# Sampling in two image halves with TensorE's part as a four-step loop, and the token norm inside the stages

## What is computed

```python
off = conv_general_dilated(x, offset_w, window_strides=(16, 16), ...)   # 2 x 256 numbers for each patch
py, px = base_y + dy, base_x + dx
y0, x0 = floor(py), floor(px)
sampled = gather(y0, x0) * (wy0 * wx0) + gather(y0, x1) * (wy0 * wx1) \
        + gather(y1, x0) * (wy1 * wx0) + gather(y1, x1) * (wy1 * wx1)
out = einsum('bhwkc,ock->bohw', sampled, Wk)                             # 192 channels
```

## Time and profile before

| | |
|---|---|
| median of 3 runs | 1202.0 us (1199.74 to 1213.42) |
| the profiled execution | 1193.13 us, span 1191.0 us, mean granted clock 0.831 |
| PE busy | 896.0 us, 75% of the span |
| DVE busy | 528.9 us, 44% |
| ACT busy | 331.6 us, 28% |
| POOL busy | 265.5 us, 22% |

### The profile page before, as it was taken

One profiled execution on the slowest core, in us unless ns is written; L12 is line 12 of the kernel. 1 busy time (PEld: TensorE's weight loads), 2 busy tenths in 40 slices (PEclk: granted clock), 3 DMA queues, 4 the chain that ended last, 5 costly groups with the idle time before them and its releaser, 6 DMA issues. The chain is left out here.

```text
span 1191.0 us, 30855 instructions
## 1 busy us (share of the span) xinstructions
PE 896.0 (75%) x13348; PEld 756.5 (64%) x13348; DVE 528.9 (44%) x1178; ACT 331.6 (28%) x668; POOL 265.5 (22%) x289
## 2 busy tenths in 40 slices
PE   8888885699729981789866595687869999286593
PEld 5676662588618971577755473565469999265472
DVE  2367672454343316555532356453641111455364
ACT  0255550221202210244541133342201111143132
POOL 2266660231022421322200101110122223200100
PEclk9899998677758995899986598785868999688598
DMA  6344436800064901000001500000518992100000
GB/s 207 66 122 128 127 96 175 223 13 1 1 195 121 208 17 57 1 2 2 2 1 38 142 4 2 2 2 1 146 48 200 238 240 38 31 3 2 1 4 22
DMA packets 56553, 87.16 MB, mean 73 GB/s; under 512 B 10390, under 2 KB 43074, under 8 KB 56414
## 3 DMA queue, kind: packets, MB, share of 16 engines
q1 hardware_dynamic: 51294, 80.26, 26.2%
q0 software_dynamic: 5120, 4.88, 2.2%
HBM read 78.35 MB, written 7.30 MB: 72 GB/s over the span
## 5 line engine op out<-in xcount | busy, mean ns | idle before, releaser
L1677 PE MATMUL ps_rows<-stage_strip,stage_hat_y 64*32 64x96 f32 x3200 | 55.0, 255 | 19.2 <-issue 18.1
L2607 DVE TENSOR_TENSOR L_ffnhid<-L_ffnact_gate,L_ffnbank_u 128x300 f32<-128x300 f32 x32 | 14.9, 467 | 117.7 <-ACT L_ffnact_gate L2625 117.7
L1745 DVE TENSOR_TENSOR stage_product<-ps_rows,stage_hat_x 128x960 f32<-128x960 f32 x40 | 46.3, 1158 | 42.6 <-PE ps_rows L1677 41.7
L1662 PE MATMUL ps_places<-stage_rel_y,stage_spread 100*64 100x128 f32 x800 | 57.9, 291 | 5.7 <-issue 3.4
L1677 PEld LDWEIGHTS ps_rows<-stage_strip,stage_hat_y 64*32 64x32 f32 x3200 | 42.0, 108 | 30.3 <-issue 30.1
L1710 POOL TENSOR_SCALAR stage_hat_x<-stage_hat_x 128x320 f32<-128x320 f32 x40 | 51.1, 1279 | 42.5 <-ACT stage_hat_x L1701 42.5
L1662 PEld LDWEIGHTS ps_places<-stage_rel_y,stage_spread 100*64 100x64 f32 x800 | 47.2, 145 | 13.4 <-issue 8.4
L1699 ACT ACTIVATE stage_hat_y<-ps_places,stage_w_minus_row 128x640 f32<-128x640 f32 x40 | 31.8, 794 | 59.8 <-PE ps_places L1662 59.8
L1718 POOL TENSOR_TENSOR stage_hat_x<-stage_rel_x,stage_w_column 128x160 f32<-128x160 f32 x80 | 37.5, 490 | 39.1 <-POOLq L1503 39.1
L1750 DVE TENSOR_REDUCE stage_samples<-stage_product 128x120 f32<-128x960 f32 x40 | 45.7, 1144 | 0.0
L2540 POOL DMA_INDIRECT stage_y_rows<-L_ffndown,stage_choice_index x16 | 25.4, 1589 | 89.2 <-ACT L_ffndown L2632 46.9
(11 more groups left out here) (432 smaller groups left out, 2244.8 us busy)
## 6 DMA issues: line engine op xcount, KB each, us to landing
stage_strip<-in_strips SPq DMA_DIRECT2D x80, 189.0 KB, 3.4
L_ffn_win<-in_L_ffn_Win SPq DMA_DIRECT2D x10, 1152.0 KB, 10.8
stage_L_ffn_win<-in_L_ffn_Win SPq DMA_DIRECT2D x6, 1152.0 KB, 10.7
L_ffnranks<-stage_ranks SPq DMA_DIRECT2D x16, 400.0 KB, 4.6
L_ffn_win<-in_L_ffn_Win SPq DMA_DIRECT2D x8, 768.0 KB, 13.5
L_ffn_wout<-in_L_ffn_Wout SPq DMA_DIRECT2D x10, 576.0 KB, 9.3
stage_L_ffn_wout<-in_L_ffn_Wout SPq DMA_DIRECT2D x6, 576.0 KB, 10.7
L_ffn_wout<-in_L_ffn_W SPq DMA_DIRECT2D x8, 384.0 KB, 13.8
```

The lines of the kernel that those rows point to most:

```text
L1662: mm = nc.tensor.matmul(ps_places[HALF_P * h:HALF_P * (h + 1), i % 2, g * P:(g + 1) * P], k.spread[:, ho * GRID + g, :], k.rel_y[:, t, h * ...
L1677: mm = nc.tensor.matmul(ps[out, i % 2, h, g * cols:(g + 1) * cols], hat_y[rows, p, g, out], strip[rows, p, :, :, left:left + WINDOW_X].rea ...
L1745: nc.vector.tensor_tensor(products(i % 2), in_psum(i % 2), weights_x(i % BUFFERS), ALU.mult).then_inc(s["multiplied"], 1)
```

## The change

1. **Order of the steps.** The 40 steps go by halves of the images, then by patch row, then by the four tiles of the half, instead of by patch row and all eight tiles. The tokens are laid out in the order of the steps.
2. **Tiles of the row places.** `convolve_y` makes tiles of 80 tokens (the 4 steps of a group) instead of 100: ten tiles instead of eight, five in each half.
3. **PE's steps as a loop.** PE's program has a loop of ten passes with four steps each instead of 40 steps written out. Its waits compare with numbers made from the loop counter. So that the instructions of a pass can be the same, SP copies the 80 x 256 places of the coming group by DMA into one of two buffers, `own_y`; PE spreads from there. The last pass spreads two steps that nobody uses. The other engines' steps stay written out.
4. **Flag.** DVE reads `far` at once, the other engines behind their steps, in the same block: the barrier and the second block are gone. The far body has 4 steps instead of 20, in one more loop.
5. **Token norm.** `finish_norm` is gone. DVE aggregates the statistics of a tile one tile later, within the last block of the layer (`count`, `end_count`), and ACT ends that block with `root`: logarithm, then exponential with scale -0.5, after asking for the table that holds both. The mean is read in place. `attention` asks for this table at its start in all its kinds.
6. GELU in four instructions instead of two.

```diff
+STEP_TOKENS = GRID * IMG_PER_TILE
+SPREADS_AHEAD = 2
+CONV_TOKENS = SAMPLE_BUFFERS * STEP_TOKENS
+CONV_TILES = ALL_TOKENS // CONV_TOKENS
...
-    steps = [(i, i // TILES, i % TILES, i % BUFFERS) for i in range(STEPS)]
+    steps = [(i, i // BUFFERS % GRID, BUFFERS * (i // (GRID * BUFFERS)) + i % BUFFERS, i % BUFFERS) for i in range(STEPS)]
...
+                    def load_places(half, q):
+                        sp.dma_start(own_y[:, half, :], k.rel_y[:, q, :]).then_inc(own_loaded[half], 16)
+                    load_places(0, 1)
+                    load_places(1, 0)
                     for i, ho, t, p in steps:
                         if i >= BUFFERS:
                             sp.wait_ge(s["rows_in_psum"], i - BUFFERS + 1)
+                        if i > BUFFERS and p % 2:
+                            sp.wait_ge(s["places"], i - 1)
+                            load_places(p // 2 ^ 1, min((i + 1) // BUFFERS, CONV_TILES - 1))
...
-                    for step in steps:
-                        if step[0] == 1:
-                            pe.wait_ge(far_known, 1)
-                        mix_rows(*step)
-                        if step[0] + 2 < STEPS:
-                            spread_places(*steps[step[0] + 2])
+                    pe.wait_ge(far_known, 1)
+                    with pe.Fori(0, CONV_TILES) as q:
+                        for p in range(BUFFERS):
+                            i = q * BUFFERS + p
+                            pe.wait_ge(s["hat_y"], i + 1)
+                            pe.wait_ge(strip_loaded[p], q * 32 + 32)
+                            pe.wait_ge(s["multiplied"], i + 1)
+                            pe.sem_inc(s["rows_free"], 1)
+                            mix_rows(p)
+                            pe.wait_ge(s["hat_y_abs"], i + 1)
+                            pe.wait_ge(own_loaded[(p + SPREADS_AHEAD) % BUFFERS // 2], q * 16 + 16)
+                            pe.sem_inc(s["places_free"], 1)
+                            coming = (p + SPREADS_AHEAD) % BUFFERS
+                            spread_places(coming, own_y[:, coming // 2, :])
+                    far = read_far(pe)
...
+                    far_steps(pe, far, far_step)
...
+class TokenNorm:
+    def count(self, dve, t):
+        tw.nc.vector.bn_stats(tw.moments[:, t, :], tw.y[:, t, :]).then_inc(self.counted, 1)
+        if t:
+            dve.wait_ge(self.counted, t)
+            tw.nc.vector.bn_aggr(tw.mean_var[:, t - 1, :], tw.moments[:, t - 1, :]).then_inc(self.aggregated, 1)
...
+    def root(self, act):
+        tw.nc.scalar.preload_act_table_set("natural_log_exp_and_others")
+        act.wait_ge(self.aggregated, TILES)
+        tw.nc.scalar.activation(tw.rstd[:], tw.mean_var[:, :, 1:2], ACT.Ln, bias=tw.eps[:]).then_inc(self.logged, 1)
+        act.wait_ge(self.logged, 1)
+        tw.nc.scalar.activation(tw.rstd[:], tw.rstd[:], ACT.Exp, scale=-0.5).then_inc(self.rooted, 1)
```

More of the change, by code:

```diff
@@ L478, in _ @@
                     store_tokens(2 * f + 2 + z)
+            norm_of.root(act)
         @block.gpsimd
@@ L517, in attention @@
     nc = tw.nc
+    norm_of = TokenNorm(tw, name)
     PAIRS = TILES // 2
@@ L1490, in offsets @@
     half_cols = ALL_TOKENS // 2
[L1491 removed]
+    half_tiles = CONV_TILES // 2
     BANKS = 8
[L1493 to L1494 removed]
+    bank_y = lambda t: t if t < half_tiles else (7, 0, 1, 2, 3)[t - half_tiles]
+    bank_x = lambda half, h: 5 + h if not half else 4 + h
     with tw.scratch(), nc.psum_tensor("ps_conv", [P, BANKS, 512], F32) as ps:
@@ L1591, in _ @@
                     reduce_x(i)
-                for t in range(half_tiles, TILES):
+                for t in range(half_tiles, CONV_TILES):
                     place_y(t)
@@ new lines, in _, with far_step @@
+                    far = read_far(pe)
+                    def far_step(i, q, t, p, wy, wx):
+                        n = B + i + 1
+                        pe.wait_ge(f["moved"], n)
+                        pe.wait_ge(f["hat_y_abs"], n - 2)
+                        for g in range(GRID):
+                            for h in range(KHALVES):
+                                mm = nc.tensor.matmul(ps_places[HALF_P * h:HALF_P * (h + 1), p % 2, g * P:(g + 1) * P], k.spread[:, p * GRID + g, :],
+                                                      own_y[:, p % 2, h * P:(h + 1) * P], start=True, stop=True)
+                        mm.then_inc(f["places"], 1)
+                        pe.wait_ge(f["hat_y"], n)
+                        pe.wait_ge(window_loaded[p], 32 // BUFFERS * (i - p + BUFFERS))
+                        pe.wait_ge(f["multiplied"], n - 2)
+                        for h in range(KHALVES):
+                            rows = slice(HALF_P * h, HALF_P * (h + 1))
+                            for g in range(GRID):
+                                mm = nc.tensor.matmul(ps[:, p % 2, h, g * cols:(g + 1) * cols], hat_y[rows, p, g, :],
+                                                      window[rows, p].rearrange("q j c x -> q (j c) x"), start=True, stop=True)
+                        mm.then_inc(f["rows_in_psum"], 1)
@@ L1764, in sample @@
-            own_y = tw.sb("own_y", [TILE_TOKENS, 2, KPOINTS])
-            B = BUFFERS
-            def far_steps(eng, step, before=None):
-                far = eng.value_load(k.far[0:1, 0:1], min_val=0, max_val=1)
-                with eng.If(far == 1):
-                    if before:
-                        before()
-                    with eng.Fori(0, COVER_Y) as wy:
-                        with eng.Fori(0, COVER_X) as wx:
-                            with eng.Fori(0, TILES // BUFFERS) as group:
-                                for ho in range(GRID):
-                                    for p in range(BUFFERS):
-                                        step((wy * COVER_X + wx) * STEPS + group * (GRID * BUFFERS) + ho * BUFFERS + p, ho, BUFFERS * group + p, p, wy, wx)
```

311 lines of the change are left out of this document (148 added, 163 removed).

## The result

| | before | after | forecast |
|---|---|---|---|
| median | 1200.9 us (1194.4 to 1213.4, 4 runs) | 1162.1 us (1152.1 to 1165.2, 4 runs) | 1170 |
| profiled execution | 1193.1 us | 1161.1 us | 1160.8 |
| mean granted clock of it | 0.831 | 0.834 | |

A forecast was written before the change was run, and what follows sets the result against it. PE's code fetch was taken to bound the sampling. 5.2 - 22 - 4.7 - 11 + 0.2 = -32.3 took the profiled 1193.1 to 1160.8 us; -32 off the 1202.0 median gave 1170, range 1157 to 1232.

The forecast's parts named there:

- The loop, -22: Sampling: with code resident, 35 steps at 2.45 us and nine jumps at 0.2 replace 109.8 us; 22 us less.
- Residence: Sampling: code of a loop pass stays on PE and is fetched only once; resident at about 2.45 us a step, chance 0.50.
- DMA share: Sampling: the share would rise from 0.45 to about 0.58 at the faster step, with the copies of places adding little.
- Row tiles, +5.2: Before the sampling: two more row tiles of six slabs, 24 records at 0.216 us each, cost 5.2 us more.
- Flag, -4.7: Between DVE's last sum and the projection: of 6.2 us, 4.7 less, taken between 5.4 and 2 less.
- The case in which the target is not near: At the flag: PE's far body lies outside the packet ahead, PE arrives 3 us behind DVE; only 2 us less.
- Norm, -11: Token norm: 1.2 us less in each of eight layers, 9.6, plus part of the gate's loads; bounds 5 and 14.
- the gate's loads: Attention's gate: a table load of 1.28 us ahead of its exponential, twice, falls away; half of it counted.
- the edits don't touch what makes that difference: Whole kernel: the median's 9 us over the profiled execution stays, so the same -32 comes off the median.
- Fetched anew: Sampling rival: each loop pass fetches its code again, 38 us more in the loop, 1231 us in all; chance 0.28.
- today's pace: Sampling rival: the jump's target is at hand but the rest is fetched, no gain from the loop, 1191 us; chance 0.10.
- another limit at 2.85 us: Sampling rival: code resident, but engines wait on each other; the loop gives 8 instead of 22, 1184 us; chance 0.12.

The follow-up runs named there:

- `strips_first`: Changed kernel, with SP issuing the first strip before the two copies of places; 1158.1 us (ratio 0.965), timed again 1151.1 us (0.961).
- `strips_early`: Changed kernel, with SP issuing the first four strips at the end of the block of the offsets; 1148.9 us (0.958), timed again 1154.3 us (0.962).
- The direct comparison: Changed kernel with the token norm of before put back; 1174.3 us, against 1159.9 us for the changed kernel beside it.
- `body_4_padded`: Changed kernel with 30 extra matmuls, read by nobody, in each step of PE's four-step loop body; 1261.0 us (one run).

## Why the prediction was right, and where it was off

**What bounds the sampling.** Right, and shown: with the code resident the step is 2.37 us and PE never stops; with the same steps written out it stops again.

**The loop, -22.** Residence was the one open fact, and it came out as taken, with the signature that was named: 80 packets (80 to 85). No row of before could show it and the prediction gave it 0.50, so the choice was a bet that came out. The size was off in two terms. A step was put at 2.45 us and each jump back at 0.2; both measured nothing beyond the stop-free step, 2.37 with the jump in it, since PE's sequencer runs ahead during the spreads. This makes 35 x 0.08 + 1.8 = 4.6 us more gain, 26.6 in all, and one step more than was counted is free of stops (36, not 35: 0.8 us). Against it stands what the forecast put at nothing: the first strip behind the two copies. The prediction followed the copy of every second step in SP's queue, but not the two ahead of the first strip, where no earlier step gives cover. `strips_first` and `strips_early` price that at 2.4 to 5 us. The net of first spread to last sum was -25.4.

**DMA share.** 0.73, not 0.58. The old 0.45 at the new pace gives 0.60. The copies are new, and the strips take longer to land; their parts in the rest were not separated. "Add little" was wrong in size, but a strip lands in 3.6 instead of 3.3 us, and no mix waited for it behind the first pass (PE has no idle time there).

**Row tiles, +5.2.** Exact in the first trace of after, and partly by chance: in ten other traces with the same row tiles and the same block of offsets the sampling starts at 51.2 to 52.7 us, 4.0 to 5.5 later than before.

**Flag, -4.7.** Measured -5.2 (-3.8 in the flag's own block, by the short jump, and -1.4 by the barrier). The case in which the target is not near was priced at 2 us of gain, with PE 3 us behind DVE; `strips_first` shows it at 1.4 us behind, a gain of 4.8. The step that failed in that branch is the start of the jump: it begins 2.3 us before DVE's end, and then has 3.3, not 4.35 us to go. The choice between both hardly mattered.

**Norm, -11.** 10.8 us by the ends of the eight layers, against 9.6 in the sum. The prediction's own pieces don't give its 1.2 us a layer: 2.5 less 0.9 to 1.0 is 1.5. The 2.5 us, from the last statistics to the root, are the first layer's alone; in the seven others the trace of before has 2.1, which the prediction doesn't show. After the change it is 0.8 in all eight, the exponential taking 0.21 us rather than 0.30 and the last aggregation ending 0.2 us behind the statistics. In the first layer 0.4 us of the 1.7 are lost again between the root and the end of the stage (1.0 where 0.6 stood). So each layer gave 1.35. The 1.2 fits the seven layers (2.1 less 0.9), not the row that it stands on. The 1.3 us for the gate's loads are not borne out (see above). The direct comparison has 14.4 us, just over the upper bound of 14, with an interval that takes in 11.

**The sum.** It met the profiled execution within 0.3 us (1160.8 and 1161.1), and that was luck: stage 0 gave 24.6 us and the ends of the eight layers 10.8, together 35.4 instead of 32.3. The stretches whose work is the same gave 3.7 back: up to its last statistics stage 3 took 8.1 us more, stages 1 and 2 took 3.9 and 2.9 less, and the others 2.5 more in sum. The medians differ by 38.8 us, 3.4 more than the edits' own 35.4. The step that failed is the last one, "the edits don't touch what makes that difference": the profiled execution of before stood 8 us under its median and that of after 1 us under its own. That the trace of before had stage 3 at a higher clock than most executions would explain it; with one trace of before this is argued, not shown. The median came out at 1162, 8 us under the forecast and inside the likeliest case's own range (1157 to 1182).

**The rivals.** Fetched anew was wrong for a body of 830 instructions, and right for one of 2,480 (1215 us). Its jump was well enough sized, 3.4 to 4.1 us against the 4.35 that was taken; what the price left out is the clock, which fell in fetched passes (0.86 and 0.73 with the body of 8). The two weaker ones, today's pace and another limit at 2.85 us, were refuted by the busy row: PE is the limit at 2.37 and DVE waits 2.5 us in 36 steps.

## What to carry to other kernels

Where an engine is idle by "issue" once per packet of its code queue, the fetch of code is the bound, and a loop can remove it, but only if its body stays on the engine: on PE 1,310 instructions did; 1,650 did so every second time, which was worth nothing (1202.3 us against 1200.6 with the steps written out); and 2,480 never, which was slower than no loop (1214.9). Read the code queue in the stretch of the repeated passes: its absence is the proof, and a body is to be sized by it. And before a profiled execution is compared with another, compare their granted clocks stage by stage; a stage whose code didn't change can move by more than the edit.

## What was not expected of the hardware

- PE keeps at least 5.1 packets of 16 KB of code over nine jumps back, at 0.21 us a jump and nothing of it on the array's path. A body of 6.5 packets survived exactly every second jump, in two traces alike.
- In the changed kernel's traces and its variants a single packet is fetched in the midst of the resident passes (at 142 us in the first trace, at 94 in the second), without a stop. In the two traces of four-step loops without it (`strips_first` and `body_4_padded`) the jump behind the loop was dear, 3.34 and 3.86 us; in the seven with it, it took 0.36 to 0.37. It was probably the page behind the loop; this is argued and not shown.
- The granted clock of a stage whose code was the same was 0.84 in one kernel and 0.88 in another, and its time 192.2 and 181.2 us, with edits upstream of it alone. The first attention took 97.2 to 103.2 us, and 98.6 and 103.2 in two traces of one kernel.
- A kernel whose pace is set by code fetch can run at a lower clock besides, for a reason that stays open: written out, the sampling ran at a granted clock of 0.88, and a step at the lower level costs 4.25 us of arithmetic instead of 2.37.
